# Vision tower: the exponential ahead of the pt and h1t copies wherever h1 is transposed, and the last transposes in the scores' banks

## What is computed

```
h    = patches(x) @ W.T                                   # 3136 tokens x 192
h1   = layernorm(h + attn1(h))                            # 12 heads of 16, causal, bias
comb = top-2 of softmax(h1 @ Wg.T + bg)                   # per token
qkv  = h1 @ Wqkv.T + bqkv + 2*(((h1 @ A + ba)*comb) @ Bm + comb @ bb)
p    = softmax(q @ k.T * 0.25)                            # per image and head, 49 x 49
out  = layernorm(h1 + (p @ v) @ Wproj.T + bproj)
```

## Time and profile before

| | |
|---|---|
| median of 3 runs | 389.62 us (389.46 to 390.89) |
| profiled execution | 389.8 us, of which span 388.0 us |
| granted TensorE clock, mean over the span | 0.996 |
| busy: TensorE / VectorE / ScalarE / GpSimd | 96% / 78% / 56% / 32% |

### The profile page before, as it was taken

The page is one execution under the profiler, slowest core; times in us unless marked ns, Lnnn a source line. Parts: engine busy times, 40 slices in busy tenths (PEclk is TensorE's granted clock), DMA queues, the critical chain, the costliest instruction groups (busy, mean ns, idle before and its releaser), DMA issues.

```text
span 388.0 us, 13738 instructions
## 1 busy us (share of the span) xinstructions
PE 373.9 (96%) x5312; PEld 328.4 (85%) x5312; DVE 303.0 (78%) x814; ACT 215.9 (56%) x692; POOL 123.1 (32%) x262
## 2 busy tenths in 40 slices
PE   5999999999999999999999999999999999999994
PEld 4888788988889888988898888888898888877983
DVE  7368677678778877988878888788898888698882
ACT  1254565655546656465655666656665575655642
POOL 1222422321234424131325223251425232424213
PEclk9999999999999999999999999999999999999998
DMA  7742521221022112420032201111011101111111
GB/s 268 231 104 61 138 55 22 68 56 50 15 68 69 25 22 69 107 56 14 16 68 66 71 8 29 17 31 25 20 18 28 30 21 18 17 27 24 26 34 39
DMA packets 49338, 20.68 MB, mean 53 GB/s; under 512 B 41262, under 2 KB 45713, under 8 KB 49274
## 3 DMA queue, kind: packets, MB, share of 16 engines
q1 hardware_dynamic: 45530, 10.43, 12.7%
q10 hardware_dynamic: 3744, 9.38, 8.1%
HBM read 12.57 MB, written 2.41 MB: 39 GB/s over the span
## 4 chain that ended last, share of the span: by engine, by line
PE 87%; DVE 4%; ACT 3%; issue 3%; POOL 2%; DMA 1%; POOLq 0%; ACTq 0%
PE ps L496 13%; PE ps L601 10%; PE ps L574 10%; PE ps L612 7%; PE ps L586 6%; PE ps L623 5%; PE ps L550 4%; PE ps L548 4%; PE ps L546 4%; PE ps L624 4%; PE ps L526 3%; PE ps L532 3%; PE ps L530 2%; PE ps L568 2%; PE ps L634 2%
## 5 line engine op out<-in xcount | busy, mean ns | idle before, releaser
L958 DVE TENSOR_REDUCE mx<-ps 113x12 f32<-113x588 f32 x64 | 48.8, 763 | 25.4 <-PE ps L574 25.0
L984 DVE TENSOR_REDUCE psum<-probs 113x12 f32<-113x588 f32 x64 | 48.5, 757 | 21.2 <-ACT probs L815 21.1
L496 PE MATMUL ps<-tokw,xs 128*128 128x192 f32 (+1 forms) x300 | 57.0, 339 | 4.6 <-DMA tokw<-in_tokw 4.6
L815 ACT ACTIVATE probs<-probs 113x588 f32<-113x588 f32 x64 | 45.4, 709 | 27.0 <-DVE probs L965 26.2
L829 ACT COPY pt<-ps 113x339 f32<-113x339 f32 x128 | 49.4, 438 | 19.2 <-PE ps L601 19.1
L445 POOL TENSOR_SCALAR shift<-mv,rstd 128x1 f32<-128x1 f32 (+1 forms) x50 | 14.3, 286 | 140.7 <-ACT rstd L864 140.7
L434 POOL TENSOR_SCALAR kbd<-k,const 64x294 f32<-64x294 f32 x64 | 34.4, 547 | 74.2 <-ACT q L808 68.4
L496 PEld LDWEIGHTS ps<-tokw,xs 128*128 128x128 f32 (+1 forms) x300 | 49.7, 195 | 7.1 <-DMA xs<-in_x 4.2
L993 DVE TENSOR_TENSOR probs<-probs,rsum 113x588 f32<-113x588 f32 x64 | 50.8, 794 | 2.2
L601 PE MATMUL ps<-const,probs 113*113 113x113 f32 x384 | 50.1, 266 | 1.6 <-DVE probs L993 1.0
L965 DVE TENSOR_TENSOR probs<-ps,mx 113x588 f32<-113x588 f32 x64 | 49.4, 771 | 2.2
(11 more groups left out here) (93 smaller groups left out, 781.5 us busy)
## 6 DMA issues: line engine op xcount, KB each, us to landing
xs<-in_x ACTq DMA_DIRECT2D x22, 384.0 KB, 3.9
vbd<-vrow SPq DMA_DIRECT2D x160, 18.4 KB
out<-o SPq DMA_DIRECT2D x24, 96.0 KB, 1.8
xs<-in_x SPq DMA_DIRECT2D x2, 384.0 KB, 6.9
tokw<-in_tokw ACTq DMA_DIRECT2D x3, 192.0 KB, 3.7
w<-in_w SPq DMA_DIRECT2D x1, 472.5 KB, 4.4
xs<-in_x SPq DMA_DIRECT2D x3, 128.0 KB, 3.4
add<-in_add SPq DMA_DIRECT2D x1, 361.5 KB, 7.7
```

The lines of the kernel that those rows point to most:

```text
L496: last = nc.tensor.matmul(ps[0:k, bank, 0:E], xs[:, b % XS, m, 0:k], tokw[:, m, :], start=(m == 0), stop=(m == KX - 1))
L815: nc.scalar.activation(p, p, ACT.Exp).then_inc(exp_ready, 1)
L958: nc.vector.tensor_reduce(mx[n % 2][:].rearrange("p (b h) -> p b h", b=2), score_view(n), AX.X, ALU.max).then_inc(mx_ready, 1)
L984: nc.vector.tensor_reduce(psum[:].rearrange("p (b h) -> p b h", b=2), probs_view(n), AX.X, ALU.add).then_inc(sum_ready, 1)
```

## The change

1. copies_late no longer asks for the absence of turns1, and where it is set take_h1 goes behind take_pt, which goes behind exponent: the order of ScalarE is exponent, take_pt, take_h1.
2. out2 of block 20 moves from slot 61 to slot 63 (with block 21); 21 and 23 go to bank 7, the others stay in bank 6.
3. The transposes of the last step (63) are issued in slot 63 instead of 64, behind weigh_values(62), into banks 0 and 1, which the scores of earlier steps used; its y goes to bank 0 too. They wait for the subtraction of step 62 and not for take_y.
4. keep_busy matmuls: 7 in place of 21, in bank 4, and they wait for the last subtraction.
5. kbd of step 63 is made ahead of normalise; layer 2 has four res buffers in place of two, the output five in place of three; in slot 64 two of three inverse deviations stand behind take_y; VectorE does out2's residual, statistics and aggregate block by block, from slot 63 on behind the scaling.

```diff
--- before.py
+++ after.py
@@ -31,7 +31,7 @@
 RING = 6 * T
 LEAD = 8
 XS = 5
-OS = 3
+OS = 5
 VR = 6
 VB = 4
 SCALE = 0.25
@@ -145,7 +145,11 @@
 routers = by_slot(ROUTED)
 qkv2s = by_slot(QKV2)
 
-OUT2 = [n + 2 + (n + 2 in [m + 2 for m in DONE1] + [len(CHAINS) - 2]) for n in DONE2]
+OUT2 = [n + 2 + (n + 2 in [m + 2 for m in DONE1]) for n in DONE2]
+
+LATE2 = [b for b in range(BLOCKS) if OUT2[b] >= len(CHAINS) - 3]
+for b in LATE2:
+    OUT2[b] = max(OUT2[b], len(CHAINS) - 1)
 out2 = by_slot(OUT2)
 norm2 = by_slot([n + (n < len(CHAINS)) for n in OUT2])
 
@@ -173,6 +177,16 @@
 def score_bank(n):
 
     return 4 if n == LAST else 0
+
+
+def turned_bank(n):
+
+    return 0 if n == LAST else 2
+
+
+def out2_bank(b):
+
+    return 7 if b in LATE2 and (b - LATE2[0]) % 2 else 6
 
 
 def moves(t):
@@ -262,7 +276,7 @@
                 self.kbd = [sb(f"kbd{n}_{u}", [64, 2, 3, T]) for u in range(2)]
                 self.vrow = [sb(f"vrow{n}_{u}", [128, E]) for u in range(VR)]
                 self.vbd = [sb(f"vbd{n}_{u}", [PP, 2, E]) for u in range(VB)]
-                self.res = [sb(f"res{n}_{u}", [128, E]) for u in range(2)]
+                self.res = [sb(f"res{n}_{u}", [128, E]) for u in range(2 * n)]
                 self.st = sb(f"st{n}", [128, 6])
                 self.pad = sb(f"pad{n}", [1, 1])
                 self.mv = sb(f"mv{n}", [128, BLOCKS, 2])
@@ -466,8 +480,9 @@
                     bias_values(b)
             for n in range(SLOTS):
 
+
                 layer, t = attention(n + 2)
-                known = bool(layer and (QKV1 if layer == 1 else QKV2)[block_of(t)] < n)
+                known = bool(layer and (QKV1 if layer == 1 else QKV2)[block_of(t)] < n) or n + 2 == LAST
                 if known:
                     block_diagonal(n + 2)
                 for b in out1(n):
@@ -590,7 +605,9 @@
 
             def transpose_probs(n, free):
                 pf = probs[n % 2][:].rearrange("p h j -> p (h j)")
-                if n > 0:
+                if n == LAST:
+                    pe.wait_ge(sub_ready, n)
+                elif n > 0:
                     pe.wait_ge(yt_ready, n)
                 if free:
                     pe.wait_ge(*free)
@@ -610,18 +627,18 @@
                     for s in range(2):
                         for g in range(3):
                             last = nc.tensor.matmul(
-                                ps[32 * g:32 * g + 32, 2, half * T + s * S:half * T + (s + 1) * S],
+                                ps[32 * g:32 * g + 32, turned_bank(n), half * T + s * S:half * T + (s + 1) * S],
                                 values[:, s, (3 * half + g) // 2, :, (3 * half + g) % 2],
                                 pt[n % 2][:, 3 * half + g, s * PB:s * PB + S], start=True, stop=True)
                 last.then_inc(pv_done, 1)
 
-            def out_project(L, w, b, slot_of, free):
+            def out_project(L, w, b, slot_of, free, bank=6):
                 k, lo = tokens(b), first_token(b)
                 if free:
                     pe.wait_ge(*free)
                 pe.wait_ge(yt_ready, slot_of[last_tile(b)] + 1)
-                nc.tensor.matmul(ps[0:k, 6, 0:E], yt[0:C, 1, lo:lo + k], w[0:C, 1, :], start=True, stop=False)
-                nc.tensor.matmul(ps[0:k, 6, 0:E], yt[:, 0, lo:lo + k], w[:, 0, :], start=False, stop=True
+                nc.tensor.matmul(ps[0:k, bank, 0:E], yt[0:C, 1, lo:lo + k], w[0:C, 1, :], start=True, stop=False)
+                nc.tensor.matmul(ps[0:k, bank, 0:E], yt[:, 0, lo:lo + k], w[:, 0, :], start=False, stop=True
                                  ).then_inc(L.proj_done, 1)
                 return L.res_ready, b + 1
 
@@ -660,11 +677,12 @@
 
             def keep_busy(count):
 
-                pe.wait_ge(L2.v_rows, BLOCKS)
+                pe.wait_ge(sub_ready, LAST + 1)
                 for _ in range(count):
-                    nc.tensor.matmul(ps[:, 7, 0:128], ident, ident, start=True, stop=True)
+                    nc.tensor.matmul(ps[:, 4, 0:128], ident, ident, start=True, stop=True)
 
             bank3 = bank4 = bank5 = bank6 = None
+            bank7 = L2.v_rows, BLOCKS
 
             for n in range(FIRST, SLOTS):
                 before, u = attention(n - 1)
@@ -678,9 +696,12 @@
                     for b in out2(n):
                         if b == 0:
                             pe.wait_ge(p2_loaded, 16)
-                        if n > LAST:
+                        if n == LAST + 2:
                             keep_busy(2)
-                        bank6 = out_project(L2, p2, b, SLOT2, bank6)
+                        if out2_bank(b) == 6:
+                            bank6 = out_project(L2, p2, b, SLOT2, bank6)
+                        else:
+                            bank7 = out_project(L2, p2, b, SLOT2, bank7, 7)
 
                 split = bool(n <= 1 and turns(n))
                 if split:
@@ -695,11 +716,10 @@
                     if n == 1:
                         pe.wait_ge(zeros_ready, 2)
                     if n == LAST:
-                        keep_busy(5)
-                    if n == LAST + 1:
-                        keep_busy(4)
-                    transpose_probs(n - 1, bank3)
-                    if n >= LAST:
+                        keep_busy(2)
+                    if n <= LAST:
+                        transpose_probs(n - 1, bank3)
+                    if n == LAST:
                         keep_busy(3)
                     if n == LAST - 1:
                         scores(L2, attention(LAST)[1], LAST)
@@ -739,12 +759,12 @@
                     weigh_values(L1, u, n - 1)
                 if before == 2:
                     weigh_values(L2, u, n - 1)
+                if n == LAST:
+                    transpose_probs(LAST, None)
                 if bare:
                     for b in out2(n):
                         if b == 0:
                             pe.wait_ge(p2_loaded, 16)
-                        if n > LAST:
-                            keep_busy(2)
                         bank6 = out_project(L2, p2, b, SLOT2, bank6)
 
                 layer, t = attention(n + 1)
@@ -875,18 +895,22 @@
                     for b in embeds(n):
                         take_h(b, 6)
 
-                copies_late = bool(len(turns(n)) + len(embeds(n)) + 2 * len(qkv2s(n)) >= 1 and not turns1(n) and n > 0)
+                copies_late = bool(turns(n) + embeds(n) + qkv2s(n)) and n > 0
                 if before and not copies_late:
                     take_pt(n - 1)
-                for b in turns1(n):
-                    take_h1(b, h1_bank(n))
+                if not copies_late:
+                    for b in turns1(n):
+                        take_h1(b, h1_bank(n))
                 if n == 0:
                     act.wait_ge(masks_ready, 1)
                 if layer and n < LAST:
                     exponent(n)
                 if before and copies_late:
                     take_pt(n - 1)
-                for b in norm2(n):
+                if copies_late:
+                    for b in turns1(n):
+                        take_h1(b, h1_bank(n))
+                for b in norm2(n)[:1]:
                     inverse_deviation(L2, b)
                 for b in qkv2s(n):
                     if not urgent(b):
@@ -910,6 +934,8 @@
                         inverse_deviation(L1, b)
                 if before:
                     take_y(n - 1, u)
+                for b in norm2(n)[1:]:
+                    inverse_deviation(L2, b)
                 if n == LAST - 1:
                     exponent(LAST)
                 if not turns(n) and not embeds(n):
@@ -995,15 +1021,16 @@
             def add_residual(L, b):
                 k = tokens(b)
                 dve.wait_ge(L.proj_done, b + 1)
-                if b >= 2:
-                    dve.wait_ge(L.ln_ready, b - 1)
-                nc.vector.tensor_tensor(L.res[b % 2][0:k], ps[0:k, 6, 0:E], h[0:k, b, :], ALU.add
+                if b >= len(L.res):
+                    dve.wait_ge(L.ln_ready, b - len(L.res) + 1)
+                bank = out2_bank(b) if L is L2 else 6
+                nc.vector.tensor_tensor(L.res[b % len(L.res)][0:k], ps[0:k, bank, 0:E], h[0:k, b, :], ALU.add
                                         ).then_inc(L.res_ready, 1)
 
             def ln_stats(L, b):
                 k = tokens(b)
                 dve.wait_ge(L.res_ready, b + 1)
-                nc.vector.bn_stats(L.st[0:k], L.res[b % 2][0:k]).then_inc(L.st_ready, 1)
+                nc.vector.bn_stats(L.st[0:k], L.res[b % len(L.res)][0:k]).then_inc(L.st_ready, 1)
 
             def ln_aggregate(L, b):
                 k = tokens(b)
@@ -1052,7 +1079,7 @@
                     subtract(LAST)
                 for b in out1(n):
                     add_residual(L1, b)
-                if n != LAST:
+                if n < LAST:
                     for b in out2(n):
                         add_residual(L2, b)
                 for b in out1(n):
@@ -1065,12 +1092,10 @@
                     sum_probs(n)
```

(14 more changed lines are left out.)

## The result

| | before | changed |
|---|---|---|
| median | 390.25 us (389.46 to 391.62, 4 runs) | 404.38 us (403.14 to 406.88, 4 runs) |
| profiled span | 388.0 us | 401.4 us |
| granted TensorE clock | 0.996 | 0.998 |

The ratio is 1.0381, with a 95% interval of 1.0336 to 1.0426. The change made the kernel 3.8% slower; 403.8 us was forecast.

The account below looks back on a forecast made before the run. TensorE was taken as the bound, busy 288.61 of 290 us in the steady part. Span 388.0 + 17.5 - 3.3 = 402.2, with 1.8 around it 404.0, less 0.2 to the median: 403.8 us; range 395 to 408.

Parts of the forecast that it names:

- The waits at bank 4: Steady part: in fourteen slots TensorE waits for the late h1t copy before project_qk2; 17.5 us, bounds 14.7 to 18.9.
- The constant of 1.74 us: project_qk2 slots: time from the subtraction's end through exponential, pt and h1t copies until TensorE can load; 1.74 us.
- Not made up later: Steady part: a stall in one slot shifts the whole next slot, so the 17.5 us stays in full.
- the half case: Rival, steady part: later slots catch up or subtractions come earlier, half of 17.5 remains; 395.1 us, chance 0.12.
- the faster one: Rival: waits at bank 4 are made up and only the tail's 3.3 us gain counts; 386.3 us, chance 0.06.
- The other slots: h1-transposing slots outside the fourteen: late copies stay hidden or wait at most 0.1 us, so no cost was added.
- taking nothing for earlier sums: VectorE's sums can start up to 0.6 us earlier; gain taken as nothing, at most 1.0 us.
- The tail: Last steps: block 20's move, earlier kbd and earlier last transposes gain 3.3 us, between 2.0 and 4.0.
- block 20's own work in slot 61: Tail: its projection leaving slot 61 saves TensorE 0.8 us; with kbd earlier, scores(63) come 0.85 us sooner.
- weigh_values, which I put at 376.75: Tail: last transposes can start at 375.15, then block 22's projection (0.85), then the last weigh_values at 376.75.
- The signs named beforehand: Fourteen h1t waits, 15 to 19 us; TensorE about 92%; slot 16 order in 1.66 us; scores(63)-to-last-residual about 2.5 us less.
- The price that I set on a lower clock: Rival: clock falls to 1.2 of 2.4 GHz after stalls, 2.13 us more per fourteen slots, 30 us; 434, chance 0.03.

Follow-up runs that it names:

- e3: Changed kernel with h1 transposed into bank 6 instead of 4 in seven project_qk2 slots that have no output projection; 394.04 us.
- e4: Changed kernel with the h1t copy placed between the exponential and the copies of pt; 394.31 us.
- e2: Kernel before with nothing but ScalarE's new order; 405.89 us.
- e5: Changed kernel with ScalarE's new order kept only in h1-transposing slots without project_qk2, the old order in the other fifteen; 387.04 us.
- e1: Changed kernel with ScalarE's old order, the tail staying as changed; 387.04 us.
- e7: e1 with block 20's output projection back in slot 61; 388.33 us.
- e9: e7 with two of the last tile's six DMAs issued by ScalarE instead of SP; 386.65 us.
- e6: e1 with two of the last tile's six DMAs issued by ScalarE, behind the last exponential, instead of SP; 385.96 us.

## Why the prediction was right, and where its terms were off

**The waits at bank 4.** Right, in place, in number (14) and in size: 17.5 us forecast, 16.9 us of waits at the loads and 16.67 us in the stretch measured. By slot the forecast was 1.00, 0.68, 1.43, 1.66 and 1.33 for 16, 8, 10, 18 and 26, the rows show 0.95, 0.65, 1.40, 1.61 and 1.29; the seven slots put level with one of these (6, 24, 34, 42, 44, 50, 52) came within 0.07 us. The constant of 1.74 us from the subtraction's end to the load was 1.71, and slots 28 and 36, taken at a mean of 1.17, have less (1.11 and 1.00). e3 shows that it is the bank, e4 that it is ScalarE's order ahead of the copy, e2 that it needs nothing else of the change.

**Not made up later.** Right. The stretch grew by as much as the waits, to 0.2 us; the half case (395) and the faster one (386) did not come.

**The other slots.** Right: e5 is level with e1. So was taking nothing for earlier sums: TensorE's wait for the scaled probabilities stayed at 1.0 us.

**The tail.** Right in kind, 2.44 us in place of 3.3, above the lower bound of 2.0. Two terms were too large. Scores(63) came 0.61 us earlier and not 0.85; e7 and e9 show that block 20's own work in slot 61 was worth 0.1, most likely because the steps behind it wait for the subtraction and pt in any case. In e7, with block 20 in slot 61, scores(63) are 0.54 earlier than before, about the 0.56 us that they waited for kbd, so nearly all of the 0.61 is kbd ahead of normalise, though no run moves kbd alone. And the step "weigh_values, which I put at 376.75", 7.7 us after scores(63), missed that the last tile's values must have landed by then: I named SP's queue nowhere in the tail. It came 8.42 us after. Taking the wait away (e6) gives 7.60, and a tail 3.27 us shorter than before, the forecast's 3.3, of which 0.62 lies ahead of scores(63) (forecast 0.85) and 2.65 behind (2.5). In the kernel before, SP's last such issue ends at 377.01 and the late transposes let weigh_values start only at 379.63, 2.6 us later and without a wait; there the order hid these DMAs, by no wide margin (e7 took 2.3 us from the last issue).

**The signs named beforehand.** Fourteen waits released by the h1t copy, 16.9 us in total, and in slot 16 exponential, pt, h1t with 1.64 us from first start to last end: as said. TensorE's share came to 93% and not 92, 373.6 us and not 371, since its busy time covers part of the waits, as above. From scores(63) to the last residual it is 1.83 us less and not 2.5: the missed wait for vbd.

**The sum.** The span was forecast at 402.2 and came to 401.4. The two misses, 0.8 too much in the steady part and 0.9 too much gain in the tail, nearly cancel; the 0.9 us of the first stretch is chance. The total is nearer than its terms deserve.

**The clock.** The granted clock stayed at 1.00 in the steady part, with fourteen idle stretches of 0.65 to 1.62 us at the loads. So the swing between levels that the Trainium skill describes (TensorE: Matmul & The Clock Gate, "A second HAM failure mode: psum-queue depth-cycling") did not appear at this share of idle time (14.1 of 304 us). The price that I set on a lower clock has no row for it: the passes it was taken from the earlier trace rows ran in a stretch whose granted clock is 1.00 too (4.10 to 7.10 us), while the first data was still arriving (DMA share 0.99), so no run shows what the lower level would have cost here.

## What to carry to other kernels

Before an instruction is moved back in an engine's order, ask for each copy behind it which buffer it frees, and who waits for that buffer next; here VectorE got the exponential for which it waited sooner, but VectorE had time to spare, and the copy pushed behind it was the one that the busiest engine needed. Where the bound engine is busy for 99% of a stretch, the price of such a wait can be worked out from the rows for each place and added up: here it came out to within 0.05 us where the slot's own rows were used, and to within 0.17 where another slot stood in. In a tail, when a chain is shortened, list what else must have arrived by its last steps, and count the time in which one queue issues its small DMAs.

## What the runs showed of the hardware

The six small DMAs that place the last tile's values took SP about 0.8 us each to issue, 4.89 us in all, and the matmul that waited for them started only 1.3 us (e1) and 2.3 us (e7) after the last was issued (375.45 to 376.76, and 375.50 to 377.83). On ScalarE's queue two such issues took 1.32 and 0.92 us (e6), and delayed nothing there: the next copies of pt start 4.87 us after scores(63), in e1 4.86.

The start of one program varies by about a us from execution to execution (first subtraction at 19.23 and 18.19 us in two of the kernel before), while the 322 us behind it repeat to 0.05.
